# Layer 0 with its 192 channels as one block of 128 and one of twice 64, instead of two blocks of 96

## The chip, the core and the metric

The kernel runs on one core of a Trainium2 chip. A core has TensorE (PE, matrix products, with PEld its loads of stationary weights), VectorE (DVE), ScalarE (ACT), GpSimd (POOL) and SyncE (SP, which here only issues transfers); each works through its own instruction list in order and waits on semaphores for the others. The metric is the time of one execution on the device in microseconds (us), lower is better. Each time given for the kernel is a median of three runs.

## The reference, cut to what matters

Sixteen images of 192 channels and 32 x 32 positions pass through four layers. Only layer 0 is touched by the change. For each image it computes, with S = 1024 tokens (the positions) and C = 192 channels:

```python
x = x + _L0_conv_ref(_gn(x), ...)          # _gn: 32 groups of 6 channels
# inside, for each image:
h = _layernorm(seq, ln_w, ln_b)                    # over the 192 channels of a token
x_in, z = jnp.split(h @ w_up + b_up, 2, axis=-1)   # 192 -> 2 x 384
x_act = silu(depthwise conv over 4 tokens of x_in)
q = x_act @ w_q; k = x_act @ w_k; v = x_in         # 12 heads of 32
hs = _mlstm_scan(q, k, v, i_pre, f_pre)            # done in 8 blocks of 128 tokens
hn = (hs normalized over a head's 32) * mh_w + mh_b
x1 = seq + (((hn + skip * x_act) * silu(z)) @ w_down + b_down)
x2 = silu(seq @ w_lin + b_lin)
y = conv_general_dilated(x1 + x2, conv2_w, 3 x 3)  # 192 -> 192 channels
y = (y - y.mean((0, 2, 3))) / sqrt(y.var((0, 2, 3)) + 1e-05) * bn_g + bn_b
```

The last line needs the mean and variance of y over all 16 images, so layers 1 to 3 start only when layer 0 is through with the last one.

## The kernel before

A tensor of 192 channels and 1024 tokens lies in memory as two blocks of 96 partitions: `xn` (the normalized input, two buffers), `h0` (input of the up projection, and under the name `yo` also the result of the 3 x 3 convolution), `yp` (the padded input of the convolution). A matmul reads up to 128 partitions and 512 tokens, so a product over 192 channels is two matmuls (k = 0, 1) per half of the tokens (h = 0, 1), and one that also has 192 output channels does this for two blocks of outputs (m = 0, 1). All of it is 32-bit; a 32-bit matmul stands in the trace as two MATMUL records, with two loads of weights.

Per image b the work of layer 0 has these stages. `enter`: mean over channels (L596), centring (DVE L625), squares (ACT L642), variance (L603), ln and exp (ACT L650, L652), scaling (DVE L629), for h = 0 and then for h = 1; then the up projection (L612, 24 matmuls). `project`: the filter over tokens (DVE L675, L678), silu (ACT L733), gates (L785), q and k (L794, 36 matmuls), and a chain of small gate operations between ACT and DVE (L759 to L770). `chunks`: 24 steps, 8 blocks of 128 tokens times 3 groups g of four heads. `norm`: on DVE and ACT (L974 to L1000). `join`: transposes (L1034), 12 DVE operations (L1060, L1062), lin (L1042, 4 outputs), down (L1048, 4 outputs), the sums into `yp` (L1068, L1072). `conv`: 72 matmuls of 96 x 96 (L1099), the copies to `yo` (ACT L1117), statistics (DVE L1124), and the store of y (SP L1130).

A step of `chunks` is, on PE, the products `pd` (L880, L883), the product `s` (L888), and then what the step before left: L847 and L852, and in the first step of a block (g = 0, except for block 0) also the update of the state (L859). In the third step (g = 2) the transposes of the next block (L868, L873) follow. ACT makes the exponentials (L957), DVE the masked copy `qd` that s needs (L926), the product L931, and in a first step the state (L908, L912). I call the steps first, middle and last, by g.

The order of the instructions on every engine is written out once by generators that are interleaved in the same way on all of them. A generator's turn ends at a `yield`; `weave` gives the next turn to the one that has had the smaller share of its turns, the first one on a tie:

```python
if b:
    weave((scan(b), 35), (conv(b - 1), 24))
else:
    run(scan(b))
if b + 1 < NB:
    weave((norm(b), 8), (enter(b + 1), 10))
```

`scan` is project (11 turns) and chunks (24 turns). So the convolution of image b - 1 is spread over the scan of image b in 24 pieces of three matmuls. Counted out, pieces 1 to 3 come after turns 1 to 3 of the scan, 4 to 7 among the q and k products, 8 after turn 11, and 9 to 24 after the chunk steps 0, 2, 3, 5, 6, 7, 9, 10, 12, 13, 15, 16, 18, 19, 21 and 22. The floating-point shares decide the tie at the very end: with 35 and 24 turns the convolution's last turn (copy to `yo`, store) comes before the scan's last turn (its last L847, L852, L944).

`enter` of image b + 1 writes `h0`, which is also `yo`, so it waits until the store of y for image b - 1 has landed. PSUM has 8 banks, handed out in turn; `hold` keeps one out of the turn (two for the accumulators of the chunks, one for the convolution).

## Time and profile before

| | before |
|---|---|
| median of 3 runs | 10595.03 us (10594.88 to 10612.04) |
| the profiled execution's own time | 10605.99 us |
| its span, first to last instruction | 10604.2 us |
| PE busy | 7902.0 us (75%) |
| DVE busy | 6391.2 us (60%) |
| mean granted TensorE clock | 0.835 of full speed |
| layer 0 ends (last store of y) | at 4502.4 us |

PE is the busiest engine, but its share is a mean over stages that differ: what a shorter matmul is worth has to be read from the stage in which it stands. Times in the rows are microseconds from the start of the span. In rows of a stretch the columns are: its bounds and length, then busy time (instructions) of PE, PEld, DVE, ACT and POOL, the granted clock as a share of full speed, the DMA share, GB/s.

### The profile page before, as it was taken

The numbers are of one execution on the slowest core, as the hardware profiler recorded it, in microseconds if no ns is written. First come the engines' busy times: TensorE is split into PE (matmuls) and PEld (weight loads), VectorE is DVE, ScalarE is ACT, GpSimd is POOL, SyncE is SP. The second block draws the span as 40 slices with busy tenths as digits, with TensorE's granted clock in tenths as the row PEclk, the third lists the DMA queues.
The fourth block names the chain that finished last, engine by engine and source line by source line (L and its number), as shares of the span: only waits on it lengthen the run. The fifth ranks groups of instructions, "written<-read, shape, count | busy, mean of one in ns | idle before, by whom it ended". The sixth has DMA issues, their size and how long they took to land.

```text
span 10604.2 us, 90359 instructions
## 1 busy us (share of the span) xinstructions
PE 7902.0 (75%) x30815; PEld 3270.5 (31%) x30958; DVE 6391.2 (60%) x11621; ACT 3859.5 (36%) x7464; POOL 1996.3 (19%) x1767
## 2 busy tenths in 40 slices
PE   7888888888888888846677667766776677667743
PEld 4444444444444444411222222222222222222211
DVE  3444444444444445343876787677777776777645
ACT  2333333333333333224444344434443444354411
POOL 0000000000000000000442244224422432243224
PEclk7899999999999999966778777887788788877866
DMA  0000000000000000010454345434543454445444
GB/s 29 4 6 6 6 6 7 6 6 7 6 6 6 6 6 4 6 60 17 139 152 116 105 143 152 116 106 142 150 118 107 140 148 116 113 140 147 113 120 147
DMA packets 289456, 776.94 MB, mean 73 GB/s; under 512 B 58086, under 2 KB 124722, under 8 KB 288612
## 3 DMA queue, kind: packets, MB, share of 16 engines
q0 software_dynamic: 92160, 453.06, 13.4%
q1 hardware_dynamic: 195524, 316.25, 11.9%
q8 instruction: 247, 4.05, 0.2%
q10 hardware_dynamic: 1312, 1.84, 0.1%
q14 instruction: 213, 1.74, 0.1%
HBM read 513.99 MB, written 96.49 MB: 58 GB/s over the span
## 4 chain that ended last, share of the span: by engine, by line
PE 47%; DVE 24%; SPq 7%; ACT 7%; DMA 6%; issue 5%; POOL 4%; ACTq 0%; DVEq 0%; POOLq 0%
PE ps L1099 8%; DVE arena L2027 6%; SPq L2373 5%; PE ps L794 5%; PE ps L888 4%; PE ps L612 4%; PE ps L2338 3%; DVE arena L1604 3%; DMA arena<-img,arena 3%; PE ps L852 3%; PE ps L1894 2%; PE ps L2349 2%; SPq L2189 2%; PE ps L2319 2%; POOL arena L2151 2%
## 5 line engine op out<-in xcount | busy, mean ns | idle before, releaser
L2027 DVE SCALAR_TENSOR_TENSOR arena<-arena 128x192 f32<-128x192 f32 x3456 | 1625.7, 488 | 324.1 <-ACT arena L2069 242.2
L2151 POOL DMA_INDIRECT arena<-img,arena x1152 | 1272.2, 1104 | 2649.7 <-DMA img<-arena 1961.0
L1099 PE MATMUL ps<-arena 96*96 96x512 f32 x2304 | 1075.7, 606 | 26.7 <-DVE arena L1072 15.0
L2338 PE MATMUL ps<-arena 128*64 128x512 f32 x3072 | 879.3, 694 | 233.4 <-DMA arena<-arena 233.0
L1604 DVE TENSOR_REDUCE arena<-ps 128x2 f32<-128x1024 f32 x768 | 892.5, 1216 | 251.4 <-PE ps L1873 245.3
L1894 PE MATMUL ps<-arena 128*64 128x512 f32 x3072 | 953.9, 719 | 2.7 <-ACT arena L1748 2.6
L1748 ACT ACTIVATE arena<-ps 128x512 f32<-128x512 f32 x1536 | 819.0, 599 | 182.7 <-PE ps L1904 180.6
L826 POOL MEMSET arena<- 76x1024 bf16 x16 | 36.2, 2262 | 4083.5 <-PE ps L852 4083.5
L957 ACT ACTIVATE arena<-ps,arena 128x128 f32<-128x128 f32 x1536 | 439.3, 369 | 868.1 <-PE ps L883 867.0
L931 DVE TENSOR_TENSOR arena<-ps,arena 128x512 f32<-128x512 f32 x384 | 265.8, 692 | 703.0 <-PE ps L888 660.0
L2069 ACT ACTIVATE arena<-arena 128x192 f32<-128x192 f32 x1152 | 502.2, 457 | 504.8 <-DMA arena<-img,arena 501.3
L1904 PE MATMUL ps<-arena 32*128 32x512 bf16 x1536 | 380.7, 455 | 314.2 <-ACT arena L1755 205.4
L888 PE MATMUL ps<-arena 128*128 128x512 f32 x768 | 436.1, 650 | 143.7 <-DVE arena L926 143.4
L2157 POOL TENSOR_TENSOR arena<-arena 128x768 f32<-128x768 f32 (+2 forms) x384 | 498.9, 1299 | 150.9 <-DVE arena L2007 128.8
L1099 PEld LDWEIGHTS ps<-arena 96*96 96x96 f32 x2304 | 359.9, 164 | 529.0 <-issue 511.3
L2300 ACT ACTIVATE arena<-ps 128x512 f32<-128x512 f32 x128 | 76.7, 599 | 1195.7 <-PE ps L2338 1195.7
L794 PE MATMUL ps<-arena 128*128 128x512 f32 x1152 | 508.6, 593 | 0.0
L2338 PEld LDWEIGHTS ps<-arena 128*64 128x64 f32 x3072 | 218.2, 154 | 680.0 <-issue 675.5
L1873 PE MATMUL ps<-arena 32*128 32x512 bf16 x1536 | 298.6, 427 | 148.9 <-DVE arena L1604 121.9
L612 PE MATMUL ps<-arena 96*128 96x512 f32 x768 | 375.8, 654 | 44.2 <-DVE arena L629 44.2
L1832 PE MATMUL ps<-arena 64*128 64x512 f32 x768 | 245.4, 718 | 198.0 <-ACT arena L1676 158.0
L2319 PE MATMUL ps<-arena 96*127 96x256 f32 (+1 forms) x1024 | 289.4, 441 | 134.8 <-DVE arena L2228 129.0
(299 smaller groups left out, 11893.9 us busy)
## 6 DMA issues: line engine op xcount, KB each, us to landing
arena<-arena SPq DMA_DIRECT2D x2048, 76.5 KB, 2.1
img<-arena SPq DMA_DIRECT2D x256, 192.0 KB, 4.1
arena<-y SPq DMA_DIRECT2D x32, 768.0 KB, 5.6
arena<-img,arena POOLq DMA_INDIRECT x1152, 4.5
arena<-x SPq DMA_DIRECT2D x16, 768.0 KB, 5.4
y<-arena SPq DMA_DIRECT2D x16, 768.0 KB, 4.3
arena<-x SPq DMA_DIRECT2D x32, 384.0 KB, 6.4
y<-arena SPq DMA_DIRECT2D x32, 384.0 KB, 3.0
```

The costliest lines, as they stand in the source:

```text
L612: i = pe.matmul(ps[:, :], W["WU"][:, k, 128 * m:128 * m + 128], self.h0[:, k, H(h)], start=k == 0, stop=k == 1)
L794: i = pe.matmul(ps[:, :], w[:, c, 128 * m:128 * m + 128], xa[:, c, H(h)], start=c == 0, stop=c == 2)
L888: pe.matmul(ps[:, :], kk[:, g, sl], self.qd[n % 3].rearrange("p a b -> p (a b)"), start=True, stop=True).then_inc(*S.mark("s_pe", b, n))
L1099: i = pe.matmul(ps[0:96, :], W["C2"][:, k, 192 * tap + 96 * m:192 * tap + 96 * m + 96], self.yp4[:, k, r0:r0 + 16, tap % 3:tap % 3 + 32], ...
L1604: dve.tensor_reduce(out, self.wides[B.at("max", b, g, n, h) // 2].rearrange("p (a b) -> p a b", a=2), AX.X, AL.max).then_inc(*S.mark("max_ ...
L1748: act.activation(self.p[n % 6], B("score", b, n)[:, :], ACT.Exp).then_inc(*S.mark("p_act", b, n))
L1894: pe.matmul(o[64 * m:64 * m + 64, :], self.va[:, tb, 64 * hd:64 * hd + 64], self.p[n % 6], start=tb == 0, stop=tb == 7).then_inc(*S.mark(" ...
L2027: i = dve.scalar_tensor_tensor(tk[:, k, :], gb[:, 192 * q:192 * q + 192], self.w4[:, q, n:n + 1], tk[:, k, :], AL.mult, AL.add)
L2069: act.activation(self.tk[n // 9 % 2][:, n % 9, :], self.g[n % 6][:, 0:192], ACT.Copy, scale=self.w4[:, 0, n:n + 1]).then_inc(*S.mark("corn ...
L2151: pool.indirect_dma_start(self.g[n % 6], None, img, bass.IndirectOffsetOnAxis(ap=ii[:, n:n + 1], axis=0)).then_inc(*S.landed(f"gather{n % ...
L2338: i = pe.matmul(ps[64 * t:64 * t + 64, :], self.dg[J % 2][:, o:o + 2, :].rearrange("p a b -> p (a b)"), win, start=n == 0, stop=n == 2)
L2373: i = sp.dma_start(self.sh[u % 3][32 * s:32 * s + 32, t, :], self.base[side][c:c + 32, o:o + 612])
```

## The change

The 192 channels of layer 0 are now held as a block A of channels 0 to 127, for both halves of the tokens, and a block B of channels 128 to 191 that lies twice: partitions 0 to 63 hold them for the first half of the tokens, partitions 64 to 127 for the second. So `xn`, `h0`, `yo`, `sq1` have the shape 128 x 3 x 512. A product over 192 channels for both halves is two full matmuls (A, h = 0 and 1) and two of 64 rows, which lie on different rows of TensorE's array (0 to 63, 64 to 127) and stand next to each other in the program. The output channels 128 to 191 of both halves lie in one bank, partitions 0 to 63 and 64 to 127: their matmuls over A have different columns, those over B different rows and different columns. The counts of PE instructions stay what they were in the up projection (24) and the convolution (72).

The order changes too. In `enter` both means come first, then both centrings, both squares, both variances. In `join` the lin products come ahead of the transposes, and the sums with them (`l`) ahead of the 12 DVE operations. ACT copies two border rows between the halves (`halo`) ahead of the convolution. The convolution has 18 pieces of one tap: nine for outputs 0 to 127 of both halves (four matmuls, two banks held), nine for outputs 128 to 191 (four matmuls of half width, one bank). The weave is (scan, 35), (conv, 18): pieces 1 and 2 come after turns 1 and 2 of the scan, 3 to 6 between turns 4 and 11, and 7 to 18 after the chunk steps 0, 2, 4 and so on to 22. Counted out in the same arithmetic, the tie at the end falls the other way: the scan's last turn comes before the convolution's last copy and store. The store and the load of an image are three transfers each. The group average of the channels takes four small matmuls instead of one, twice per image. The statistics for the batch norm are brought into the old layout by four transfers after the last image.

The diff, cut to its core; lines that go are mostly left out, since they stand in the functions above:

```diff
+        for m in range(2):
+            g[:, 2 * k + m, :] = (chan[k][:, None] // 6 == chan[m][None, :] // 6) * (1 / 12 if k else 1 / 6)
+    c["G4"] = g
+    c["ONE"] = np.full((128, 128), 1 / 192, np.float32)
...
+        for m in range(2):
+            for k in range(2):
+                i = pe.matmul(ps[:, m:m + 1], self.C["G4"][:, 2 * k + m, :], v[:, k:k + 1], start=k == 0, stop=k == 1)
...
-        self.h0 = self.yo = ar([96, 2, 1024])
-        self.sq1 = ar([96, 1024])
-        self.lnr = ar([96, 512])
...
+        self.xn = [ar([128, 3, 512]) for _ in range(2)]
+        self.h0 = self.yo = ar([128, 3, 512])
+        self.sq1 = ar([128, 3, 512])
+        self.sqf = self.sq1[0:12, 0:2, :].rearrange("p a b -> p (a b)")
+        self.lnr = self.sl = ar([128, 3, 512])
...
+        sp.dma_start(xn[:, 0:2, :], src[0:128, :].rearrange("c (h n) -> c h n", h=2)).then_inc(*S.landed(f"x_in{b % 2}", b, 0))
+        for h in range(2):
+            sp.dma_start(xn[64 * h:64 * h + 64, 2, :], src[128:192, H(h)]).then_inc(*S.landed(f"x_in{b % 2}", b, 1 + h))
...
     def pe_enter(self, pe, b):
...
+        mean = []
         for h in range(2):
             ps, free = B.take(("mean", b, h), ("ln_dve", b, h, "cen", 1))
             pe.wait_ge(*free)
...
+            mean.append(ps)
+        pe.wait_ge(*S("gn0_dve", b, "out", 1))
+        for h in range(2):
+            pe.matmul(mean[h][:, :], one, xn[:, h, :], start=True, stop=False)
+        for h in range(2):
+            pe.matmul(mean[h][:, :], one[64 * h:64 * h + 64, :], xn[64 * h:64 * h + 64, 2, :], start=False, stop=True).then_inc(*S.mark("ln_pe", b, h, "mean"))
+        yield
+        yield
+        for h in range(2):
             ps, free = B.take(("var", b, h), ("ln_act", b, h, "ln"))
             pe.wait_ge(*free)
             pe.wait_ge(*S("ln_act", b, h, "sq", 1))
...
+            pe.matmul(ps[:, :], one, sq1[:, h, :], start=True, stop=False)
+            pe.matmul(ps[:, :], one[64 * h:64 * h + 64, :], sq1[64 * h:64 * h + 64, 2, :], start=False, stop=True).then_inc(*S.mark("ln_pe", b, h, "var"))
             yield
         pe.wait_ge(*S("ln_dve", b, 1, "n", 1))
         for m in range(6):
+            up = []
             for h in range(2):
                 ps, free = B.take(("up", b, m, h), ("up_act", b, m, h))
                 pe.wait_ge(*free)
...
+                up.append(ps)
+            for h in range(2):
+                pe.matmul(up[h][:, :], W["WU"][:, 0, 128 * m:128 * m + 128], h0[:, h, :], start=True, stop=False)
+            for h in range(2):
+                r = slice(64 * h, 64 * h + 64)
+                pe.matmul(up[h][:, :], W["WU"][r, 1, 128 * m:128 * m + 128], h0[r, 2, :], start=False, stop=True).then_inc(*S.mark("up_pe", b, m, h))
             yield
...
     def dve_enter(self, dve, b):
...
+        dve.wait_ge(*S(f"y_out{b % 2}", b - 2, 2))
+        dve.wait_ge(*S("conv_dve", b - 2, 2))
         for h in range(2):
...
+            r, ps = slice(64 * h, 64 * h + 64), B("mean", b, h)
             dve.wait_ge(*S("ln_pe", b, h, "mean"))
...
+            dve.tensor_tensor(h0[:, h, :], xn[:, h, :], ps[:, :], AL.subtract).then_inc(*S.mark("ln_dve", b, h, "cen", 0))
+            dve.tensor_tensor(h0[r, 2, :], xn[r, 2, :], ps[r, :], AL.subtract).then_inc(*S.mark("ln_dve", b, h, "cen", 1))
+            yield
+        for h in range(2):
+            r = slice(64 * h, 64 * h + 64)
             dve.wait_ge(*S("ln_act", b, h, "rstd"))
...
+            dve.tensor_tensor(h0[:, h, :], h0[:, h, :], lnr[:, h, :], AL.mult).then_inc(*S.mark("ln_dve", b, h, "n", 0))
+            dve.tensor_tensor(h0[r, 2, :], h0[r, 2, :], lnr[r, h, :], AL.mult).then_inc(*S.mark("ln_dve", b, h, "n", 1))
             yield
         yield from skip(6)
...
+            r = slice(64 * h, 64 * h + 64)
+            act.wait_ge(*S("ln_dve", b, h, "cen", 0))
+            act.activation(sq1[:, h, :], h0[:, h, :], ACT.Square).then_inc(*S.mark("ln_act", b, h, "sq", 0))
+            act.wait_ge(*S("ln_dve", b, h, "cen", 1))
+            act.activation(sq1[r, 2, :], h0[r, 2, :], ACT.Square).then_inc(*S.mark("ln_act", b, h, "sq", 1))
+            yield
+        act.wait_ge(*S("join_dve", b - 2, "y", 2))
+        for h in range(2):
             act.wait_ge(*S("ln_pe", b, h, "var"))
...
+            act.activation(lnr[:, h, :], B("var", b, h)[:, :], ACT.Ln, bias=self.C["CV"][:, 0:1]).then_inc(*S.mark("ln_act", b, h, "ln"))
             act.wait_ge(*S("ln_act", b, h, "ln"))
...
+            act.activation(lnr[:, h, :], lnr[:, h, :], ACT.Exp, scale=-0.5).then_inc(*S.mark("ln_act", b, h, "rstd"))
             yield
...
     def pe_join(self, pe, b):
...
+        lin = []
+        for n in (0, 2, 1):
+            ps, free = B.take(("lin", b, n), ("join_act", b, n))
+            pe.wait_ge(*free)
+            lin.append(ps)
+        both = [slice(0, 64), slice(64, 128)]
+        for h in range(2):
+            pe.matmul(lin[h][:, :], W["WL"][:, 0, 0:128], xn[:, h, :], start=True, stop=False)
+        for h, r in enumerate(both):
+            pe.matmul(lin[h][:, :], W["WL"][r, 1, 0:128], xn[r, 2, :], start=False, stop=True).then_inc(*S.mark("join_pe", b, "lin", 2 * h))
+        for h, r in enumerate(both):
+            pe.matmul(lin[2][r, :], W["WL"][:, 0, 128:192], xn[:, h, :], start=True, stop=False)
+        for h, r in enumerate(both):
+            i = pe.matmul(lin[2][r, :], W["WL"][r, 1, 128:192], xn[r, 2, :], start=False, stop=True)
+        i.then_inc(*S.mark("join_pe", b, "lin", 1))
         pe.wait_ge(*S("norm_dve", b, "out"))
         for h in range(2):
...
+        for n in range(3):
+            ps, free = B.take(("down", b, n), ("join_dve", b, "y", n))
+            pe.wait_ge(*free)
+            pe.wait_ge(*S("join_dve", b, "gate", 5 if n else 2))
+            for c in range(3):
+                if n == 1:
+                    for h, r in enumerate(both):
+                        i = pe.matmul(ps[r, :], W["WD"][:, c, 128:192], qt[:, c, H(h)], start=c == 0, stop=c == 2)
+                else:
+                    i = pe.matmul(ps[:, :], W["WD"][:, c, 0:128], qt[:, c, H(n // 2)], start=c == 0, stop=c == 2)
+            i.then_inc(*S.mark("join_pe", b, "down", n))
     def dve_join(self, dve, b):
...
+        for n in range(3):
+            dve.wait_ge(*S("join_act", b, n))
+            dve.scalar_tensor_tensor(sl[:, n, :], xn[:, block[n], :], W["BD"][:, n % 2:n % 2 + 1], sl[:, n, :], AL.add, AL.add).then_inc(*S.mark("join_dve", b, "l", n))
...
+        for n, inner in enumerate((self.ypa[:, 1:17, 1:33], self.ypb[:, 1:17, 1:33], self.ypa[:, 17:33, 1:33])):
+            dve.wait_ge(*S("join_dve", b, "l", n))
+            dve.wait_ge(*S("join_pe", b, "down", n))
+            dve.wait_ge(*S("conv_pe", b - 1, 2))
+            if n == 1:
+                dve.wait_ge(*S("halo", b - 1, 1))
+            dve.tensor_tensor(inner, r16(B("down", b, n)[:, :]), r16(sl[:, n, :]), AL.add).then_inc(*S.mark("join_dve", b, "y", n))
...
+    def act_join(self, act, b):
...
+        for n in (0, 2, 1):
+            act.wait_ge(*S("join_pe", b, "lin", n))
+            act.wait_ge(*S("ln_dve", b + 1 if b + 1 < self.NB else b, 1, "n", 1))
+            act.table(ACT.Silu)
+            act.activation(self.sl[:, n, :], B("lin", b, n)[:, :], ACT.Silu, bias=W["BL"][:, n % 2:n % 2 + 1]).then_inc(*S.mark("join_act", b, n))
+        act.wait_ge(*S("join_dve", b, "y", 1))
+        act.activation(ypb[0:64, 17, 1:33], ypb[64:128, 1, 1:33], ACT.Copy).then_inc(*S.mark("halo", b, 0))
+        act.activation(ypb[64:128, 0, 1:33], ypb[0:64, 16, 1:33], ACT.Copy).then_inc(*S.mark("halo", b, 1))
...
+    def pe_conv(self, pe, b):
...
+            ps, free = B.hold(("conv", b, h), ("conv_act", b, h))
+            pe.wait_ge(*free)
+            out.append(ps)
+        pe.wait_ge(*S("join_dve", b, "y", 2))
+        pe.wait_ge(*S("halo", b, 1))
+        for tap in range(9):
+            y, x = divmod(tap, 3)
+            w = slice(192 * tap, 192 * tap + 128)
             for h in range(2):
...
+                pe.matmul(out[h][:, :], W[:, 0, w], self.ypa[:, 16 * h + y:16 * h + y + 16, x:x + 32], start=tap == 0, stop=False)
+            for h, r in enumerate(both):
+                i = pe.matmul(out[h][:, :], W[r, 1, w], self.ypb[r, y:y + 16, x:x + 32], start=False, stop=tap == 8)
+                if tap == 8:
+                    i.then_inc(*S.mark("conv_pe", b, h))
+            yield
+        for h in range(2):
+            B.drop(("conv", b, h))
+        ps, free = B.hold(("conv", b, 2), ("conv_act", b, 2))
+        pe.wait_ge(*free)
+        for tap in range(9):
+            y, x = divmod(tap, 3)
+            w = slice(192 * tap + 128, 192 * tap + 192)
+            for h, r in enumerate(both):
+                pe.matmul(ps[r, :], W[:, 0, w], self.ypa[:, 16 * h + y:16 * h + y + 16, x:x + 32], start=tap == 0, stop=False)
+            for h, r in enumerate(both):
+                i = pe.matmul(ps[r, :], W[r, 1, w], self.ypb[r, y:y + 16, x:x + 32], start=False, stop=tap == 8)
+            if tap == 8:
+                i.then_inc(*S.mark("conv_pe", b, 2))
+            yield
+        B.drop(("conv", b, 2))
...
+        for n in range(3):
+            if n != 1:
+                yield from skip(9)
...
     def sp_conv(self, sp, b):
...
+        yield from skip(18)
+        sp.wait_ge(*S("conv_act", b, 2))
+        sp.dma_start(dst[0:128, :].rearrange("c (h n) -> c h n", h=2), self.yo[:, 0:2, :]).then_inc(*S.landed(f"y_out{b % 2}", b, 0))
+        for h in range(2):
+            sp.dma_start(dst[128:192, H(h)], self.yo[64 * h:64 * h + 64, 2, :]).then_inc(*S.landed(f"y_out{b % 2}", b, 1 + h))
...
-                weave((scan(b), 35), (conv(b - 1), 24))
+                weave((scan(b), 35), (conv(b - 1), 18))
...
+            dve.wait_ge(*S("bn_in", 3))
...
+            sp.wait_ge(*S("conv_dve", NB - 1, 2))
+            own = L0.stats.rearrange("p n b s -> p (n b) s")
+            for n, (dst, src) in enumerate(((stats_keep[:, 0], own[0:96, 0:2 * NB]), (stats_keep[0:32, 1], own[96:128, 0:2 * NB]),
+                                            (stats_keep[32:96, 1, 0:NB], own[0:64, 2 * NB:3 * NB]), (stats_keep[32:96, 1, NB:2 * NB], own[64:128, 2 * NB:3 * NB]))):
+                sp.dma_start(dst, src).then_inc(*S.landed("bn_in", n))
```

## Rows read from the trace of the kernel before

**Rows 1.** The page of the profile, busy time of each engine
```profile
PE 7902.0 (75%) x30815; PEld 3270.5 (31%) x30958; DVE 6391.2 (60%) x11621; ACT 3859.5 (36%) x7464; POOL 1996.3 (19%) x1767
```

**Rows 2.** Timeline of the SP queue: start, us, engine, line
```profile
1388.44 0.31 SPq L1130 DMA_DIRECT2D y<-arena  x1
...
1661.52 0.31 SPq L1130 DMA_DIRECT2D y<-arena  x1
```

**Rows 3.** Timeline of PE, paired matmuls; columns as above, rows*columns of the tile
```profile
1465.76 2.80 PE L785 MATMUL ps<-arena 128*64 128x512 f32 x12
...
5178.70 1.08 PE L1818 MATMUL ps<-arena 128*64 128x512 f32 x4
5179.71 1.13 PE L1832 MATMUL ps<-arena 64*128 64x512 f32 x4
5180.77 1.08 PE L1818 MATMUL ps<-arena 128*64 128x512 f32 x4
```

**Rows 4.** Groups by line, PE, the last convolution (4439.6 to 4502 us)
```profile
L1099 PE MATMUL ps<-arena 96*96 96x512 f32 x144 | 62.0, 592 | 0.9 <-DVE arena L1072 0.9
```

**Rows 5.** The chain that ended last: start, us, what
```profile
1413.07 23.33 PE ps L612 x48
...
1482.64 2.58 PE ps L1099 x6
```

**Rows 6.** Timeline of ACT at the end of an image's scan
```profile
1387.72 0.69 ACT L1117 ACTIVATE arena<-ps,arena 96x512 f32<-96x512 f32 x1
...
1389.80 0.50 ACT L944 ACTIVATE arena<-ps 128x396 f32<-128x396 f32 x1 [1.39 <-PE ps L852]
```

**Rows 7.** Timeline of the enter stage; in brackets: idle before, releaser
```profile
1392.84 1.28 DVE L625 TENSOR_TENSOR arena<-arena,ps 96x512 f32<-96x512 f32 x2 [1.45 <-DMA y<-arena]
...
1394.93 3.70 PE L603 MATMUL ps<-arena 96*96 96x512 f32 x4 [3.40 <-ACT arena L642]
...
1400.05 1.29 DVE L629 TENSOR_TENSOR arena<-arena 96x512 f32<-96x512 f32 x2 [5.93 <-ACT arena L652]
...
1401.26 3.34 DVE L977 TENSOR_REDUCE arena<-arena 128x96 f32<-128x3072 f32 x1
```

**Rows 8.** Timeline of the join stage on DVE
```profile
1436.88 0.75 DVE L1060 SCALAR_TENSOR_TENSOR arena<-ps,arena 128x512 f32<-128x512 f32 x1 [0.78 <-PE ps L1034]
...
1444.60 0.69 DVE L1062 TENSOR_TENSOR arena<-arena 128x512 f32<-128x512 f32 x1
...
1457.06 0.69 DVE L1072 TENSOR_TENSOR arena<-ps,arena 96x512 f32<-96x512 f32 x1 [1.18 <-PE ps L1048]
```

**Rows 9.** Timeline of PE, chunk steps 4, 5 and 11 to 14
```profile
1562.58 1.10 PE L888 MATMUL ps<-arena 128*128 128x512 f32 x2
...
1565.44 1.13 PE L888 MATMUL ps<-arena 128*128 128x512 f32 x2 [0.28 <-DVE arena L926]
...
1598.83 1.13 PE L888 MATMUL ps<-arena 128*128 128x512 f32 x2
...
1602.92 1.10 PE L888 MATMUL ps<-arena 128*128 128x512 f32 x2 [0.80 <-DVE arena L926]
...
1608.82 1.10 PE L888 MATMUL ps<-arena 128*128 128x512 f32 x2
...
1613.87 1.08 PE L888 MATMUL ps<-arena 128*128 128x512 f32 x2
```

**Rows 10.** Image 0: timeline of PE, stretch of its chunks
```profile
184.28 1.10 PE L888 MATMUL ps<-arena 128*128 128x512 f32 x2 [2.56 <-DVE arena L926]
...
163.10:287.00 123.90, 101.60 (x446) 74.01 (x453) 54.36 (x178) 32.44 (x104) 0.00 (x0) 0.66 0.00 1
```

**Rows 11.** Images 11 and 12: one line's instructions, one stretch
```profile
L888 PE MATMUL ps<-arena x48: 592/620/697, 3181.4 to 3298.5; 128*128 128x512 f32 x48
...
L888 PE MATMUL ps<-arena x48: 592/620/697, 3454.8 to 3573.6; 128*128 128x512 f32 x48
...
3455.80:3459.20 3.40, 3.40 (x6) 1.13 (x5) 1.48 (x5) 0.00 (x0) 0.00 (x0) 0.50 0.00 0
```

239 lines of the change are left out of this document (109 added, 130 removed).

## The prediction, made before the changed kernel was run

> **What bounds the kernel.** I read the page first: PE is busy for 75% of the span [rows 1], far from all of it, so the question is in which stages a shorter matmul shortens the image. Two stores of y give the period of an image in layer 0: 1661.52 - 1388.44 = 273.08 us [rows 2]; fifteen such periods and the last image are 4500 of the 10604 us, and nothing after layer 0 changes. The chain of waits shows what a period is made of: the up projection, 23.33 us, all PE [rows 5]; the join, from the end of the up projection (1413.07 + 23.33 = 1436.40) to the last sum into yp (1457.75), 21.35 us [rows 5, 8]; project, where four pieces of the convolution stand between the q and k products and lengthen the chain by 2.58 us each [rows 5]; the chunks, 117.1 us from the first s to the last [rows 11]; and enter, from the first centring (1392.84) to the up projection (1413.07), 20.23 us of ping-pong between DVE, ACT and PE [rows 5, 7].
>
> In the chunks the three kinds of step differ, and the whole forecast hangs on it [rows 9]. A middle step takes 2.86 us without a piece of the convolution and 5.05 with one: PE bounds it. A last step takes 4.09 without one, and 1602.92 shows why it does not hide a piece either: the 0.80 us that PE waits for DVE's copies come behind the piece, after the next block's transposes; with a piece I take 4.09 + 2.58 = 6.67. A first step takes 5.90 with a piece (1602.92 to 1608.82), and image 0, which has no convolution beside it, shows that it takes as long without one: there PE sits idle 2.56 us before the next s, for DVE, which has the state to update [rows 10]. So a piece behind a first step is free, one behind a middle step costs about 2.2, one behind a last step 2.6 us.
>
> **What a paired matmul costs.** The twelve L785 records, pairs on different columns, take 2.80 us, as six records of 0.43 (62.0 / 144, rows 4) do with the tail: such pairs run wholly at once [rows 3]. L1832 (64 rows by 128 columns, two tiles of rows, 32-bit: the form of the new B matmuls) alternates with column pairs: 5178.70 to 5179.71 to 5180.77, 2.07 us for two pairs, against 4 x 0.43 = 1.72 if they ran on [rows 3]. So a pair costs two record times, 0.86, plus about 0.18 for each change between the forms. That is the dearest part of the promise: each new piece changes form twice or three times. TensorEngine Tiling (Array Packing), Key Properties, in the Trainium skill says that changing the tiling mode drains TensorE; it gives no figure, and the trace agrees, with 0.35 us for two changes; without a drain a period would be some 7 us shorter.
>
> A tap of the first nine pieces is four full records, a pair and two changes: 1.72 + 0.86 + 0.36 = 2.94. One of the last nine is a column pair and a diagonal pair (64 x 64) with three changes: 1.72 + 0.54 = 2.26. Before, a piece was 2.58. No row shows a diagonal pair; bounds are 0.86, if both run at once as the two nearer kinds do, and 1.72, one after the other. I take 0.86: the tiles share neither rows nor columns.
>
> **The change, part by part, per image.**
>
> Chunks. Pieces now stand behind steps 0, 2, 4 ... 22: four behind first steps (free), four behind middle ones, four behind last ones. Before, of sixteen, eight stood behind first steps, six behind middle ones and two behind last ones. Priced by kind: before 6 x 2.19 + 2 x 2.58 = 18.3. After: the first-nine kind behind step 2 (2.94) and step 4 (2.55), the other kind behind three middle steps (1.87 each) and three last ones (2.26 each): 17.9. Step 0, with no state to update, grows by 0.4. Sum 0.0: four pieces fewer, 30% less PE work in the pieces, and nothing gained, because those that go are the free ones. The two copies to yo now come together on ACT, and the group averages add 12 small records; both within 1 us, taken as 0.
>
> The clock. Four first steps per image (3, 9, 15, 21) now have no piece and so an idle gap of about 2.6 us on PE; now no gap there is above 0.8 in [rows 9]. In image 0, where every first step has that gap, the granted clock of the chunks is 0.66, while PE was at work for 101.6 of 123.9 us [rows 10]. One stretch at 1.2 GHz at the start of image 12's chunks (clock 0.50 for 3.4 us) makes them 118.8 us long instead of 117.1 [rows 11]. So a gap costs 1.7 us if it brings one such stretch, and 3.4 if it brings two; in image 0, 0.66 means 68% of 123.9 us at 1.2 GHz, some 10 us for each of its eight first steps, so more than one is likely where no piece follows. Here a piece of full matmuls follows each gap. I take 2.1, near the measured 1.7: +8.4 per image; and 0 as the bound if the gap, with pieces on both sides, does not bring the clock down.
>
> Project. Pieces 1 and 2 hide under the filter on DVE (before: 1 to 3), 3 to 6 stand on the chain, four as before, but longer: 4 x (2.94 - 2.58) = 1.4. PE waits longer ahead of the second half of the gates (two pieces instead of three in front), so more of it starts at 1.2 GHz: 1.1, bounds 0 and 2. Together +2.5. The piece that now stands in the gate chain was hidden there anyway.
>
> End of the scan. Before, ACT copies the last conv output at 1387.72 and the store goes out at 1388.44, while PE still does the last chunk. Now the scan's last turn is ahead: L944 at 1389.80 to 1390.30, then the copy to 1391.0: the store leaves 2.6 us later, and centring waits for it (1392.84, idle until the DMA) [rows 2, 6, 7]. Queued behind that centring are norm's reductions and all of enter. +2.6. The store as three transfers: two more issues of 0.31, each transfer smaller; taken as 0, bounds -0.5 and +1.
>
> Enter. Count from the first centring, at 0. Squares done 2.1 (1394.93 - 1392.84), variance h = 0 (3.70 as now, and a change of form) 6.0, ln and exp 1.4 as now (1400.05 - 1398.63) 7.4, scaling 8.7. DVE meanwhile has centred h = 1 and done L977 (3.34). The variance of h = 1 ends at 9.7 and its exp at 11.1, hidden behind norm's next operation on DVE (the same 3072 elements, priced as L977), which ends at 12.05; scaling 13.35. Now it is 20.23, since h = 1 starts only after L977 [rows 7]. -6.9.
>
> Up projection: six times 2.94 plus the 2.7 that it now loses by starting at the lower clock (23.33 - 48 x 0.43): 20.3. -3.0.
>
> Join, from the end of the up projection. Lin is 1.72 + three pairs 2.58 + four changes 0.7 = 5.0; its last silu (priced as the copy L1117, 0.69) ends at 5.9, `l` for it and the next, about 0.65 each, at 7.2. Only then come the twelve DVE operations, 8.4 us together ((1445.29 - 1436.88), rows 8): 15.6. The second and third down product, 2.58 each, wait for the last gate: 21.0; latency and sum: 21.9. PE idles 3.6 us ahead of the first down product and restarts at the lower clock, which the slack before 15.6 hides all but some 0.5. So 22.4 against 21.35: +1.0. Where PE was the bound, with 40 records, it now waits for DVE; the 12 record times that lin and down save are gone.
>
> **The sum.** Scans with a convolution: 15 x (0.0 + 8.4 + 2.5 + 2.6) = +202. Enter and up: 16 x -9.9 = -158, less 2 for image 0, whose enter has no norm between: -156. Joins: 15 x 1.0, and the last, where lin hides under norm, -5: +10. The last convolution, alone: 9 x (2.94 + 2.26) = 46.8 instead of 62.0 [rows 4]: -15. The four transfers of statistics on the chain, one round of about 3.5 (a store takes 4.4 to land, rows 2 and 7): +4. Sum +45: the profiled execution's 10605.99 us (1.8 of them outside the span) becomes 10651; the median of the runs shown is 11 us below it, so I forecast 10640 us.
>
> **Rivals.**
> The clock holds (faster). If a gap of 2.6 us with pieces on both sides doesn't bring the clock down, 15 x 8.4 = 126 go: 10514. For it: PE is busy at both ends of such a gap, unlike in image 0. Against it: the gap is as long as those in image 0. It decides the sign where the gaps cost less than 4.0 us per image instead of 8.4 (45 + 21 = 66 us over fifteen images), so where fewer than two of the four bring the clock down. Chance 0.25.
> No change that can be measured: two or three of the four gaps are costly, and cancel against enter and the up projection. Within 21 us (0.2%, about what a measurement of this kernel can tell from no change). Chance 0.18.
> Diagonal pairs run one after the other. Six of the nine pieces stand behind middle and last steps, 0.86 each, three behind first ones, 0.3 each; 15 x 6.1 = 91, lin 13, last convolution 8: 10752. TensorEngine Tiling (Array Packing), Gotcha 1, in the Trainium skill says that different row tiles can't access the same PSUM bank at once, and both halves of a diagonal pair write one bank. The rows against: the two halves of L785 share a bank and run at once, but they are tiles of columns only [rows 3]. Chance 0.14.
> The forecast itself, with gaps from 1.7 to 3.4 us: 10616 to 10718. Chance 0.43.
>
> Its own range is 10616 to 10718. The range over all cases, from the clock that holds to the serial pairs, is 10510 to 10755. Faster 0.25, same 0.18, slower 0.57.
>
> **What would show it.** Period of the stores of y about 277.5 instead of 273.08. First steps without a piece still 5.9 us apart with 2.6 idle ahead of the next s; granted clock of the chunks clearly below that of before, in the middle steps behind them. Up projection near 20 us, enter near 13.4. First of the twelve DVE operations of the join about 7.2 us after the last up matmul. L944 ahead of the last conv copy on ACT. Two diagonal matmuls starting within some 10 ns, or 0.86 apart. The forecast is wrong if the clock of the chunks stays at 1.00, if pieces behind last steps hide after all, or if the banks held by the convolution (two instead of one) make PE wait in steps 0 to 5, which I priced at nothing because every bank that comes round was read a step earlier.

## The result, and the profile after

The changed kernel takes 10792.99 us (median of 4 runs, 10785.31 to 10794.71); the kernel before, on the same chip, 10603.53 us (4 runs). The ratio is 1.0177, 95% interval 1.0159 to 1.0194. The forecast was 10640 us with a range up to 10755: the direction was right, the size was not, +189 us instead of +45.

The page of the changed kernel, busy time of each engine, answers to [rows 1]:

```profile
span 10793.0 us, 90733 instructions
PE 7825.2 (73%) x31008; PEld 3170.4 (29%) x31150; DVE 6351.5 (59%) x11557; ACT 3835.3 (36%) x7464; POOL 1973.3 (18%) x1768
```

PE's busy time fell by only 77 us, although the convolution has 27% less to do (44.98 us alone instead of 62.0, below). The timeline of the SP queue answers to [rows 2]:

```profile
1440.41 0.33 SPq L1256 DMA_DIRECT2D y<-arena  x1
...
1727.13 0.33 SPq L1256 DMA_DIRECT2D y<-arena  x1
```

The period is 286.72 us instead of 273.08: 13.64 more, fifteen times, 205 us. Outside the periods the last convolution gives 17 us back. The period can be cut at six points that the traces of both kernels have, in us; px is the DVE instruction that multiplies the scores (L931, now L1025), one for each of the 24 steps, taken at its end:

| stretch | before | after | difference | forecast |
|---|---|---|---|---|
| chunks, first to last product px | 116.92 | 135.86 | +18.94 | +8.4 |
| last px to first centring | 4.21 | 6.26 | +2.05 | +2.6 |
| enter | 20.23 | 12.94 | -7.29 | -6.9 |
| up projection | 23.33 | 19.55 | -3.78 | -3.0 |
| join | 21.34 | 22.07 | +0.73 | +1.0 |
| last sum to next first px (project) | 87.04 | 90.03 | +2.99 | +2.5 |

Five of the six terms are within 0.8 us, and together 1.5 us lower than forecast. The whole miss lies in the chunks. The px of image 4, and PE's work between the first and the last; the windows' columns are as in [rows 10], the granted clock third from the end:

```profile
L1025 DVE TENSOR_TENSOR arena<-ps,arena x24: 690/690/692, 1301.3 to 1437.2; 128x512 f32<-128x512 f32 x24
...
1302.00:1437.80 135.80, 115.72 (x578) 68.50 (x584) 55.98 (x184) 34.33 (x110) 0.00 (x0) 0.84 0.00 1
```

The same window of the kernel before:

```profile
1271.70:1388.60 116.90, 109.22 (x567) 67.20 (x574) 57.00 (x187) 34.98 (x111) 0.00 (x0) 1.00 0.00 1
```

The clock fell from 1.00 to 0.84: 0.16 x 135.8 = 21.7 us of full speed were not granted, more than the 18.9 us lost. Where it falls shows in PE's timeline behind a first step that has no piece (in brackets: idle before, releaser):

```profile
1317.56 0.92 PE L953 MATMUL ps<-arena 128*128 128x132 f32 x6
1318.31 0.38 PE L974 MATMUL ps<-arena 128*128 128x512 bf16 x1
1318.53 0.39 PE L977 MATMUL ps<-arena 76*128 76x128 bf16 x4
1321.48 2.05 PE L982 MATMUL ps<-arena 128*128 128x512 f32 x2 [2.56 <-DVE arena L1020]
1323.32 0.65 PE L941 MATMUL ps<-arena 128*128 128x132 f32 x2
1323.76 1.75 PE L946 MATMUL ps<-arena 128*128 128x33 f32 x8
1325.32 3.76 PE L1210 MATMUL ps<-arena 128*128 128x512 f32 x4
1329.02 1.91 PE L1212 MATMUL ps<-arena 64*128 64x512 f32 x4
1330.86 0.39 PE L974 MATMUL ps<-arena 128*128 128x512 bf16 x1
1331.09 0.39 PE L977 MATMUL ps<-arena 76*128 76x128 bf16 x4
1331.31 1.08 PE L982 MATMUL ps<-arena 128*128 128x512 f32 x2
...
1320.50:1330.70 10.20, 9.22 (x20) 4.50 (x20) 2.26 (x10) 0.00 (x0) 0.00 (x0) 0.50 0.00 0
```

The gap of 2.56 us is the forecast one. Behind it the scores take 2.05 instead of 1.10 us, and the next piece 5.54 from its start to that of L974 instead of 2.98; only at 1331 are the durations those of 2.4 GHz again. The last row is a window: 10.2 us at a granted clock of 0.50, which is 1.2 GHz, from the last microsecond of the gap on, with PE busy for 9.22 of them. At the other three such gaps of this image the clock is 0.50 for 10.2, 6.8 and 10.2 us (from 1357.9, 1395.5 and 1426.2). The gaps themselves were forecast; stretches as long as this behind them were not.

There is one more, which was not forecast: from 1344.3 to 1347.7, behind a gap of 1.63 us ahead of the scores at 1342.43. That first step (step 6) has a piece, but one of the half-width kind, 2.02 us long, where the pieces of before were 2.58; it no longer fills the time for which PE waits there.

### The profile page after: what moved, and what is told of

Read it like the earlier page. It is cut to its first block, busy times and chain, and to the rows that moved or that the text cites. A ratio compares the mean times of both kernels' runs of the same rounds, so it can differ in the third digit from the quotient of the medians.

```text
span 10793.0 us, 90733 instructions
## 1 busy us (share of the span) xinstructions
PE 7825.2 (73%) x31008; PEld 3170.4 (29%) x31150; DVE 6351.5 (59%) x11557; ACT 3835.3 (36%) x7464; POOL 1973.3 (18%) x1768
## 3 DMA queue, kind: packets, MB, share of 16 engines
q1 hardware_dynamic: 198916, 316.40, 11.5%
## 4 chain that ended last, share of the span: by engine, by line
PE 46%; DVE 24%; SPq 7%; ACT 7%; DMA 6%; issue 5%; POOL 4%; DVEq 0%; ACTq 0%; POOLq 0%
SPq L2506 5%; DVE arena L2160 5%; PE ps L888 5%; PE ps L982 5%; PE ps L946 3%; PE ps L2471 3%; DVE arena L1737 3%; DMA arena<-img,arena 3%; PE ps L1210 2%; PE ps L2482 2%; POOL arena L2284 2%; SPq L2322 2%; PE ps L702 2%; PE ps L2452 2%; PE ps L2027 2%
## 5 line engine op out<-in xcount | busy, mean ns | idle before, releaser
L1025 DVE TENSOR_TENSOR arena<-ps,arena 128x512 f32<-128x512 f32 x384 | 265.4, 691 | 925.5 <-PE ps L982 862.6
L982 PE MATMUL ps<-arena 128*128 128x512 f32 x768 | 523.6, 769 | 331.6 <-DVE arena L1020 328.1
L888 PE MATMUL ps<-arena 128*128 128x512 f32 x1152 | 506.7, 596 | 0.0
L946 PEld LDWEIGHTS ps<-arena 128*128 128x128 f32 x3072 | 442.0, 221 | 0.0
L946 PE MATMUL ps<-arena 128*128 128x33 f32 x3072 | 435.4, 290 | 0.0
L2006 PE MATMUL ps<-arena 32*128 32x512 bf16 x1536 | 299.3, 427 | 147.9 <-DVE arena L1737 120.8
L2037 PEld LDWEIGHTS ps<-arena 32*128 32x128 bf16 x1536 | 76.6, 94 | 959.9 <-ACT arena L1881 649.1
```

Source lines behind the costliest of these rows:

```text
L888: i = pe.matmul(ps[:, :], w[:, c, 128 * m:128 * m + 128], xa[:, c, H(h)], start=c == 0, stop=c == 2)
L946: i = pe.matmul(po[:, 33 * h:33 * h + 33], px[:, 128 * j:128 * j + 128], v1[:, 33 * h:33 * h + 33], start=False, stop=j == 3)
L982: pe.matmul(ps[:, :], kk[:, g, sl], self.qd[n % 3].rearrange("p a b -> p (a b)"), start=True, stop=True).then_inc(*S.mark("s_pe", b, n))
```

## The experiments

Three theories. **Clock**: the gaps without a piece cost the 18.9 us, through the clock. **Placing**: pieces behind last steps and the two held banks cost it, and the clock is a by-product. **Order, not layout**: with pieces where PE is idle, the new layout is faster than the old one. Most experiments change only the order in which the stages are issued. In place of `weave` stands

```
def lay(plan, end, scan, conv):
    for n in range(1, 36):
        next(scan, None)
        for _ in range(plan.get(n, 0)):
            next(conv, None)
        if n == end:
            next(conv, None)
    run(scan)
    run(conv)
```

Turns 1 to 11 are project (4 the gates, 5 to 10 the q and k products, 11 the gate transposes), turn 12 + n is step n of the chunks. The diffs write a plan in words and are cut to the lines that matter. The first lines of those of experiments 3 and 2 are what `weave` does in the changed kernel (its end is 36: never ahead of the scan's) and in the one before (35).

All results. Ratio to the kernel before on the same chip with its 95% interval; period, chunks (first to last px) and clock in the chunks from the profiled execution, image 4:

| kernel | ratio | period | chunks | clock |
|---|---|---|---|---|
| kernel before | 1 | 273.08 | 116.92 | 1.00 |
| changed kernel | 1.0177 (1.0159-1.0194) | 286.71 | 135.86 | 0.84 |
| 1 constant matmuls, wrong steps | 1.0211 (1.0194-1.0228) | 290.12 | 137.43 | 0.88 |
| 2 before, four gaps | 1.0177 (1.0160-1.0194) | 286.66 | 130.42 | 0.88 |
| 3 pieces behind first steps | 0.9825 (0.9808-0.9841) | 262.82 | 111.79 | 0.95 |
| 4 store earlier | 1.0078 (1.0061-1.0094) | 279.87 | 131.47 | 0.88 |
| 5 constant matmuls in the gaps | 0.9982 (0.9973-0.9992) | 273.07 | 120.83 | 0.97 |
| 6 q and k pieces moved | 1.0089 (1.0072-1.0106) | 279.89 | 133.78 | 0.86 |
| 7 new layout, own order | 0.9750 (0.9692-0.9808) | 252.59 | 107.82 | 0.92 |
| 8 old layout, own order | 1.0038 (1.0024-1.0053) | 275.45 | 113.74 | 0.99 |
| 9 as 8, mended | 0.9766 (0.9749-0.9782) | 256.37 | 107.63 | 0.99 |
| 10 as 7, refined | 0.9633 (0.9617-0.9649) | 249.19 | 105.57 | 0.95 |
| 11 two of four gaps filled | 1.0071 (1.0054-1.0088) | 279.90 | 128.17 | 0.90 |

One thing in the column of periods was not foreseen. Apart from experiments 8 and 9 they do not lie just anywhere: they differ from one another by whole multiples of 3.41 us, to within 0.03 (249.19, 252.59, 262.82, 273.08, 279.89, 286.71, 290.12). Experiment 2 changes between 286.66 (image 4) and 283.39 (image 3), about a step lower. So a price per gap that is read from a period is known only to such a step divided by the number of gaps, and a saving of a microsecond or two can show as nothing or as 3.4. Why the periods stand in steps is open. The prices below are therefore also given by the medians.

### 1 and 5: the gaps filled with work that computes nothing

```
                 pe.wait_ge(*free)
+                if b and n % 6 == 3:
+                    for _ in range(10):
+                        pe.matmul(ps[:, :], self.idb, self.mkb, start=True, stop=True)
                 pe.wait_ge(*S("qd", b, n))
```

In the fifth experiment the condition is `n % 6 == 4`.

> The changed kernel, with ten bf16 matmuls of constants (128x512) written into the bank of the next scores before step 3, 9, 15 and 21 of the chunks, where no piece of the convolution stands; they are overwritten at once. Only work is added, nothing moves. Clock theory: the chunks grew by 18.9 us per image (116.9 to 135.9 from the first px to the last) because each of these idle gaps brings the clock down for 7 to 10 us behind it; in the chunks of one image 41 us are at 1.2 GHz, 37 of them behind the four gaps, and half of that time is lost if PE bounds them. So 12 to 18 us per image come back: 180 to 270 us faster than the changed kernel, 10520 to 10610 us, and the chunks last 118 to 124 us. Placing theory (the pieces behind last steps and the two held banks cost the time, the clock is a by-product): the added matmuls lie in idle time, so 0 to 30 us slower than the changed kernel, chunks still 136 us.

Neither theory's number came: 1.0211, worse than the changed kernel. Its timeline shows that I had put the matmuls a step too early. They run ahead of step 3's scores, where PE was not idle, and the gap ahead of step 4's is still there:

```profile
1317.68 2.10 PE L983 MATMUL ps<-arena 128*128 128x512 bf16 x9
...
1325.43 1.10 PE L985 MATMUL ps<-arena 128*128 128x512 f32 x2 [2.56 <-DVE arena L1023]
```

So it does not test the theories as it was meant to. Such work on the path costs: 290.12 - 286.71 = 3.4 us of the period. But four times 2.1 us were put on the path and the chunks grew by only 1.6, with the clock at 0.88 instead of 0.84, so some of it came back. The same at the right steps:

> As the first experiment, but with the ten constant bf16 matmuls at the right place: ahead of the scores of steps 4, 10, 16 and 22, where the trace of the first one shows PE idle for 2.56 us (it waits for DVE, which has just updated the state), and not ahead of steps 3, 9, 15 and 21, where PE had no idle time and the added 2.1 us were paid. Clock theory: the idle time is filled, the clock stays up behind it, chunks 118 to 128 us instead of 135.9, 120 to 270 us faster than the changed kernel: 10520 to 10670. Placing theory: 0 to 30 us slower than the changed kernel.

Measured 0.9982; the changed kernel was 1.0177. Forty added matmuls per image take 0.0195 off the ratio, 207 us of 10603.53 (the two ratios come from different chips, each against the kernel before on its own). The gap is closed to 0.31 us and the scores behind it run at full speed:

```profile
1276.69 2.32 PE L983 MATMUL ps<-arena 128*128 128x512 bf16 x10
1279.33 1.12 PE L985 MATMUL ps<-arena 128*128 128x512 f32 x2 [0.31 <-DVE arena L1023]
...
1259.80:1380.60 120.80, 110.34 (x628) 66.41 (x627) 56.03 (x185) 34.34 (x110) 0.00 (x0) 0.97 0.00 1
```

The clock theory holds, for 15.0 of the chunks' 18.9 us. The placing theory falls as the main cause: at most 3.9 us are left to it, and the clock of 0.97 still stands for up to 0.03 x 120.8 = 3.6 of those. The timeline shows where: from 1336.5 to 1343.3 the clock is 0.50, and from the scores of step 15 to those of step 16 it takes 8.66 us, where the same stretch from step 3 to step 4 takes 5.80. No gap of 2.56 us stands ahead of it, only one of 1.10, some under 1, and twice the small matmuls of the group average (L500, eight records each); which of these brings the clock down there was not tested.

### 2: the gaps made in the kernel before

```
-PLAN: one piece behind turns 1 2 3 5 6 8 9 11 12 14 15 17 18 19 21 22 24 25 27 28 30 31 33 34
+PLAN: one piece behind turns 1 2 3 5 6 8 9 12 14 17 18 19 22 24 25 28 30 31 34, five behind 11
```

> The kernel before, layout and pieces of the convolution unchanged, but the four pieces behind steps 3, 9, 15 and 21 of the chunks stand instead in the idle stretch of PE ahead of the first chunk (between the transposes of the gates and the matmuls behind them, 14 us with one piece in it). A piece that was free goes to a place that is free. Clock theory: the four gaps appear in the kernel before as well and the chunks grow from 116.9 by 12 to 18 us; ahead of them 1 to 2 us come back since PE is no longer idle there: 150 to 250 us slower than before, 10750 to 10850. Placing theory: no piece stands at a dearer place than before, so 0 to 30 us faster than before.

Measured 1.0177, by chance the same number as the whole change, with nothing of the new layout in it. The chunks grew to 127.4 to 131.8 us (130.42 in image 4). Timeline and window:

```profile
1325.69 1.78 PE L888 MATMUL ps<-arena 128*128 128x512 f32 x2 [2.56 <-DVE arena L926]
1327.27 0.65 PE L847 MATMUL ps<-arena 128*128 128x132 f32 x2
1327.71 1.76 PE L852 MATMUL ps<-arena 128*128 128x33 f32 x8
...
1306.20:1436.60 130.40, 113.08 (x541) 69.64 (x548) 57.02 (x186) 34.33 (x110) 0.00 (x0) 0.88 0.00 1
```

Four gaps add 286.66 - 273.08 = 13.6 us to the period of image 4, 3.4 each, the number by which the fifth lowers it; in image 3 they add 10.3. By the medians a gap costs (10796.23 - 10616.34) / 60 = 3.0 us here, net of what the moved pieces give back ahead of the chunks, and 207 / 60 = 3.4 in the fifth. The clock is 0.50 for 6.8 us behind each of the four, not for 10. A piece that hides behind a first step is not only free: taken away, it costs more than it takes (2.58).

### 11: two of the four gaps filled

```
-                if b and n % 6 == 4:
+                if b and n in (10, 22):
```

> As the fifth (constant matmuls in idle gaps of PE in the chunks), but only ahead of steps 10 and 22, not ahead of 4 and 16. All four gave back 13.6 us per image, 3.4 each. If each gap has its own price, two give 7 us per image: 100 us faster than the changed kernel, ratio to before 1.008. Rival: the gaps act on each other (one that stays open brings the clock down at another moment and makes the next one dearer or cheaper), and the result lies clearly off the middle, below 1.003 or above 1.013.

Measured 1.0071, a period of 279.90: 6.8 us below the changed kernel's, half of 13.6. The prices of these gaps add up, as far as periods that move in steps of 3.41 us can show it: it is two steps of four. By the medians it is (1.0177 - 1.0071) x 10603.53 / 30 = 3.7 us a gap.

### 3: a piece behind every first step

```
-PLAN: one piece behind turns 1 2 4 6 8 10 12 14 16 18 20 22 24 26 28 30 32 34
+PLAN: one piece behind turns 1 2 4 6 8 10 12 15 18 21 22 24 25 27 28 30 31 33
```

> The changed kernel with the twelve pieces that stand in the chunks behind steps 0, 3, 6, ... 21 (every first step) and 10, 13, 16, 19 (middle ones), instead of behind every second step; nothing else moves. Clock theory: chunks without a gap, 18 us back, and by my prices for the places another 9 (three first-nine kind pieces at 0.4 and four of the other kind at 1.9, against 17.9): chunks 109 to 117 us, 290 to 400 us faster than the changed kernel, 10390 to 10500. Placing theory: only the 9 us: 135 us faster, 10650, with the clock of the chunks near 0.83 as now.

Measured 0.9825, chunks 111.79 us. Same work, same layout, six of the twelve places in the chunks changed: 3.5% faster than the changed kernel. Of the 24.1 us that the chunks lost, the clock explains at most 21.7 - 0.05 x 111.8 = 16.1. In experiment 5 the chunks gave back 15.0 us for 18.1 of regained full speed; at that rate it is 13.3 here. So 8 to 11 are left for the places, where my prices per step kind gave 9.

### 4: the store ahead of the scan's last turn

```
-                lay(PLAN, 36, scan(b), conv(b - 1))
+                lay(PLAN, 35, scan(b), conv(b - 1))
```

> The changed kernel with what follows the last piece of the convolution (the copy of the last output, its statistics, the stores) issued before the scan's last piece instead of behind it; nothing else moves. My term for this in the prediction was 2.6 us per image; the traces show 6.26 against 4.21 us from the last px to the first centring. If the term is right, 2.1 us per image come back: 30 us faster than the changed kernel, 10760. Rival: ACT's copy then waits for the last piece, which PE does late, and holds up the exp of the last step: no difference, or up to 15 us slower.

Measured 1.0078, 1.0% faster than the changed kernel, three times the term. From the last px to the first centring it is 4.42 instead of 6.26 us, 1.84 and as expected. But the chunks are 4.4 us shorter too, their clock 0.88 instead of 0.84. Everything behind the store comes 2 us earlier, and though the gaps of over 1 us are the same to 0.01 us, the clock behind them is not: behind the first it is 0.50 for 3.4 us instead of 10.2, behind the one of 1.63 us it stays up, and behind the other three nothing changes. I had no term for that; why the shift does it is open.

### 6: the q and k pieces moved

```
-PLAN: one piece behind turns 1 2 4 6 8 10 12 14 16 18 20 22 24 26 28 30 32 34
+PLAN: one piece behind turns 1 2 12 14 16 18 20 22 24 26 28 30 32 34, four behind 11
```

> The changed kernel with the four pieces of the convolution that stand between and behind the q and k products put into the idle stretch of PE behind the second group of gate transposes (14.18 us long); the chunks keep their places. The trace puts each at 2.97 us on the chain that leads to the gates, so 11.9 us per image come back from there, and the clock is up at the start of the chunks, 1 to 3 us more: 180 to 220 us faster than the changed kernel, 10570 to 10610. Rival: the q and k products are not what the gate chain waits for (ACT's and DVE's own work on the gates is), and the pieces were hidden: 0 to 30 us faster.

Measured 1.0089, 93 us below the changed kernel, half of what I expected. Project became 4.7 us shorter, not 11.9. Its timeline shows what the pieces had covered:

```profile
1491.61 15.72 PE L888 MATMUL ps<-arena 128*128 128x512 f32 x36
1512.07 17.18 PE L888 MATMUL ps<-arena 128*128 128x512 f32 x36 [4.74 <-ACT arena L849]
```

PE now waits 4.74 us in the middle of the products for ACT to empty a bank, and the second half starts at the lower clock (17.18 instead of 15.72 us). So the pieces had in part covered a wait, and only the rest of their time had been on the path.

### 7 and 8: each layout with an order of its own

```
+seventh: one piece behind turns 1 2 12 15 18 21 24 25 27 30 33, two behind 3, five behind 11; end 35
+eighth: one piece behind turns 1 2 12 15 18 19 21 22 24 25 27 28 30 31 33 34, three behind 3, five behind 11; end 35
```

> The changed kernel's layout with an order of its own: four pieces ahead of the gates, five in the idle stretch behind the gate transposes, one behind each first step of the chunks, one behind step 13, and what follows the last piece issued before the scan's last piece. The third experiment gave 24 us per image against the changed kernel, the fourth 6.5, the q and k products stand for 11.9, some of it overlapping: 10200 to 10300 us, and faster than both kernels. Rival: the stretches filled here were not on the path, then about the 10430 us of the third.

> The kernel before with the same kind of order for its 24 pieces: five ahead of the gates, five in the idle stretch, one behind each first step of the chunks, six behind middle steps. Nothing of the new layout. Four pieces leave the q and k chain (10.3 us per image), two leave last steps of the chunks (5.2), the clock behind the gates comes up (1 to 2): 10330 to 10400 us. What the seventh is faster than this one is the worth of the layout by itself: by my terms enter 7.3, up 3.8 and the shorter pieces, less the join and three piece lengths, 5 to 12 us per image, 75 to 180 us.

The seventh gave 0.9750, faster than both kernels but short of the 10200 to 10300 us; its four runs lie from 10317.68 to 10456.01 us, and why they differ is open. The eighth gave 1.0038 where I expected about 0.977. Its timeline:

```profile
1526.58 5.44 PE L1099 MATMUL ps<-arena 96*96 96x512 f32 x6
1541.45 9.02 PE L1099 MATMUL ps<-arena 96*96 96x512 f32 x14 [9.44 <-ACT arena L1117]
```

The old layout computes four outputs one after the other, each in a bank. The piece that begins the second one waits 9.44 us for ACT's copy of the first, which my order issued behind ACT's work on the gates. The idle stretch that the pieces were to fill was spent waiting, and they then ran on the path, at first at the lower clock (the second row ends with the view, at 1550).

### 9 and 10: both orders mended

```
+ninth: one piece behind turns 1 2 7 8 12 15 18 21 22 24 25 27 28 30 31 33, three behind 3, five behind 11; end 35
+tenth: one piece behind turns 1 2 7 12 15 18 21 24 25 27 30 33, two behind 3, four behind 11; end 35
```

> The kernel before, in an order without the mistake of the eighth experiment, where PE waited 9.4 us for a bank because ACT's copy of the first output was issued behind ACT's gate work: five pieces ahead of the gates, one behind each of the third and fourth q and k products, five in the idle stretch behind the gate transposes, one behind each first step of the chunks and behind steps 10, 13, 16 and 19. Against the order of before, two pieces leave the q and k chain (5.2 us per image) and two last and two middle steps of the chunks lose theirs (9.5): 10 to 17 us per image, 150 to 250 us faster than before, ratio 0.976 to 0.986. Rival: the clock falls in new places or another bank is late: ratio 0.99 to 1.00.

> As the seventh, but one piece stands behind the third q and k product, where its trace shows PE idle for 4.75 us, and four instead of five in the idle stretch behind the gate transposes, where the fifth ran 1 to 2 us beyond the time at which the gates were ready. 2 to 5 us per image: 30 to 75 us faster than the seventh, ratio to before 0.968 to 0.973. Rival: no difference, since the filled 4.75 us are followed by a wait for ACT all the same.

Measured 0.9766, within its range, and 0.9633 (10217.77 us against 10606.04), below its range of 0.968 to 0.973; both on one chip. The tenth is the fastest. It differs from the seventh by one piece, which shortens the period by 3.4 us (priced at 2 to 5); that the median fell by more comes from the scatter of the seventh's runs. The piece now stands in the 4.75 us idle time between the q and k products, which falls to 1.96:

```profile
1379.30 1.89 PE L1210 MATMUL ps<-arena 128*128 128x512 f32 x4
1381.11 1.13 PE L1212 MATMUL ps<-arena 64*128 64x512 f32 x4
1384.20 17.41 PE L888 MATMUL ps<-arena 128*128 128x512 f32 x36 [1.96 <-ACT arena L849]
```

The difference of the two, 1.33% of 10606 us or 141 us, is what the layout is worth with the second order tried for each. Neither order is shown to be the best: with the first order tried for the new layout (the seventh, 0.9750) the advantage over the ninth is 0.16% and not clear of noise. The tenth's chunks still run at a clock of 0.95, the ninth's at 0.99. It is the same layout that made the kernel 1.8% slower in the order it came with.

## Why the prediction was wrong, point by point

- **The clock: the step that failed.** I named the four first steps without a piece, the gap of 2.6 us and its effect. I then took "2.1, near the measured 1.7" per gap, +8.4 per image, reasoning that full matmuls behind the gap would bring the clock back sooner than in image 0. The runs put the gap at 3.0 to 3.7 us (experiments 2, 5 and 11), about my upper bound; inside the chunks four of them are 15.0 us instead of 8.4. The single stretch of image 12 [rows 11] was the wrong model: it has 3.4 us at 1.2 GHz, while three of the four gaps bring 10.2 and one 6.8. Image 0 [rows 10] was the nearer row: some 10 us of lower clock per first step. That full matmuls behind a gap bring the clock back sooner is what failed: the piece that starts at 1325.32 ran at 1.2 GHz to 1330.7, all but its end.
- **Chunks otherwise, taken as 0.0: the second term that was mis-sized.** With 3.4 us a gap the forecast's own sum gives 10718, still 75 us short. 3.9 us per image, 59 us, remain in the chunks once the gaps are filled. They come with a clock of 0.97, which leaves almost nothing for the places; 2.9 of them lie in the one stretch at 1336.5 of experiment 5, which has the group averages' small matmuls ahead of it, a term taken as 0. That a piece behind a first step is free whatever its length was also too simple: the half-width pieces leave a gap of 1.63 us. Neither was tested by itself.
- **That a piece is free behind a first step, about 2 us behind a middle and 2.6 us behind a last one.** Consistent with experiment 3, where 8 to 11 us were left beside the clock's share and these prices give 9.
- **Project.** +2.99 against +2.5. The statement that four pieces stand on the chain was too strong: experiment 6 took them away and got 4.7 us for 11.9.
- **End of the scan.** +2.05 against +2.6; ACT does L1038 at 1439.31 and then the copy L1242 at 1439.70, as forecast. The secondary effect on the clock (experiment 4) was not foreseen.
- **Enter, up projection, join.** -7.29, -3.78 and +0.73 against -6.9, -3.0 and +1.0. The timeline of DVE shows the order that was worked out, the second scaling at 1455.60, 11.5 us after the first centring:

```profile
1444.11 0.69 DVE L717 TENSOR_TENSOR arena<-arena,ps 128x512 f32<-128x512 f32 x1 [0.84 <-issue]
...
1446.74 3.35 DVE L1071 TENSOR_REDUCE arena<-arena 128x96 f32<-128x3072 f32 x1
1451.12 0.69 DVE L723 TENSOR_TENSOR arena<-arena 128x512 f32<-128x512 f32 x1 [1.03 <-ACT arena L746]
...
1455.60 0.68 DVE L723 TENSOR_TENSOR arena<-arena 128x512 f32<-128x512 f32 x1
```

- **Pairs.** A tap of the first nine takes 2.98 us (1215.00 - 1212.03 in the trace), forecast 2.94; one of the last nine 2.02 where they follow each other in the last convolution, forecast 2.26, since only two changes of form fall on a tap there, not three. A change is (2.02 - 1.72) / 2 = 0.15 us, taken as 0.18. Diagonal pairs, for which no row existed, run at once. The groups of the last convolution answer to [rows 4]:

```profile
L1210 PE MATMUL ps<-arena 128*128 128x512 f32 x36 | 17.9, 618 | 0.8 <-DVE arena L1180 0.8
L1212 PE MATMUL ps<-arena 64*128 64x512 f32 x36 | 10.2, 641 | 0.0
L1224 PE MATMUL ps<-arena 128*64 128x512 f32 x36 | 9.7, 618 | 0.0
L1226 PE MATMUL ps<-arena 64*64 64x512 f32 x36 | 9.7, 614 | 0.0
```

- **The last convolution.** 44.98 us against 62.0, -17.0; forecast -15. The statistics' transfers came to 9.84 - 5.08 = +4.8 us between the first issue of the last store of y and the load that comes next (L1285, now L1418); forecast +4.
- **The rivals.** That the clock holds was wrong in the trace (0.84) and by experiment 2. That diagonal pairs run one after the other was wrong: 36 records of L1226 in 9.7 us are 0.27 each, and a record alone takes 0.43. TensorEngine Tiling (Array Packing), Gotcha 1, in the Trainium skill says that different row tiles cannot access one PSUM bank at once; here the two halves of a diagonal pair write one bank and overlap, so the measurement decides against it for this form. The banks held by the convolution made PE wait nowhere in the chunks: its 19.4 us of waits there are all for DVE's L1020.

## What to carry to other kernels

When PE is not the bound everywhere, count a filler's place before its length: a piece of work that sits in an idle gap can be worth more than its own duration, because it keeps the clock of what follows; removing or shortening filler work is a change with a price, and constant matmuls in the gap are a quick test of it. After a change of the number or length of interleaved pieces, lay them out anew against the idle stretches in the trace, and look at which bank, and whose copy, each piece waits for. Judge a new layout by both kernels in an order of their own: here the order that came with it hid behind a loss of 1.8% a gain of 1.3% (by the best order found for each).

## What the runs showed of the hardware

- Behind an idle gap of 2.56 us came a stretch at 1.2 GHz of 10.2 us, in which PE was busy for 9.22; behind the other gaps of this length it was 3.4, 6.8 or 10.2 us (changed kernel, experiments 2 and 4). Four such gaps cost 13.6 us of a 273 us period.
- A shift of the work by 2 us, with the same gaps, changed the mean clock of the chunks from 0.84 to 0.88, their length by 4.4 us and the period by 6.8 (experiment 4; 1.84 of these are the shift itself). Times of single gaps can't be carried over to better than that.
- Two matmuls on 64 rows and 64 columns each, on the diagonal, ran at once while writing different partitions of one bank: nine such pairs of 32-bit matmuls over 512 columns took 9.7 us, 1.08 a pair, where the records of full tiles, one after the other, would give 1.72.
- Three DMAs (512, 128 and 128 KB) in place of one store of 768 KB did not delay what waits for it: from the first issue to the first centring 3.70 us, 4.40 before.
